# A gated recurrence after linear attention: steps 4 to 7 and the output stage cut in halves of the tokens

## The reference, cut to what matters

```python
# per batch t: x1 = layernorm(x + attention(x)), attention with elu(.)+1 features
def step(c, xt):
    ft = sigmoid(xt @ wf.T + c @ uf.T + bf)
    it = sigmoid(xt @ wi.T + c @ ui.T + bi)
    gt = tanh(xt @ wc.T + c @ uc.T + bc)
    return ft * c + it * gt, None
c_final, _ = lax.scan(step, c0, x1)
h = tanh(einsum('tbi,oi->tbo', x1, wo) + c_final @ uo.T + bo)   # for every tile t
return layernorm(x1 + h)
```

## Time and profile before

| what | value |
|---|---|
| time, median of 3 runs | 106.99 us (106.97 to 107.19) |
| profiled execution, its own time | 107.27 us |
| its span in the trace | 105.2 us |
| PE busy | 92.5 us (88%) |
| DVE busy | 79.5 us (76%) |
| ACT busy | 62.1 us (59%) |
| POOL busy | 40.6 us (39%) |

### The profile page before, as it was taken

How to read it: one execution, slowest core, us unless ns; L and a number is a source line. 1 busy time by engine, 2 the same in 40 slices (tenths; PEclk the granted TensorE clock), 3 DMA queues, 4 the chain that set the end, 5 groups by cost and what they waited for, 6 DMA issues and landing times.

```text
span 105.2 us, 1758 instructions
## 1 busy us (share of the span) xinstructions
PE 92.5 (88%) x570; PEld 78.5 (75%) x570; DVE 79.5 (76%) x225; ACT 62.1 (59%) x115; POOL 40.6 (39%) x59
## 2 busy tenths in 40 slices
PE   6998999889999999999999999999999999991000
PEld 4878779469688968878887888898898899991000
DVE  3325398998999995898689589389592648999950
ACT  1326675349395684676659374374753735799731
POOL 2006277607247149009306604304300002786780
PEclk9999999999999999999999999999999999999855
DMA  1869994000000000000000000000000000034453
GB/s 44 284 250 406 387 386 176 6 0 3 0 0 0 0 0 0 9 0 0 0 0 6 0 0 0 0 0 0 3 0 6 0 0 0 0 142 161 179 211 108
DMA packets 4372, 7.28 MB, mean 69 GB/s; under 512 B 491, under 2 KB 1292, under 8 KB 4364
## 3 DMA queue, kind: packets, MB, share of 16 engines
q1 hardware_dynamic: 3932, 6.85, 17.7%
q10 hardware_dynamic: 432, 0.33, 1.1%
HBM read 5.08 MB, written 2.10 MB: 68 GB/s over the span
## 4 chain that ended last, share of the span: by engine, by line
PE 72%; DVE 18%; POOL 3%; ACT 3%; issue 2%; POOLq 0%; DVEq 0%; ACTq 0%
PE ps_ctx L326 7%; PE ps_k L307 7%; PE ps_ctx L346 6%; PE ps_q L317 5%; DVE stats L663 5%; DVE x L790 4%; PE ps_f L296 4%; PE ps_x L357 3%; POOL rstd L247 2%; DVE x L675 2%; PE ps_f L370 2%; PE ps_f L376 2%; PE ps_c L371 2%; PE ps_c L370 2%; PE ps_c L376 2%; PE ps_i L371 2%
## 5 line engine op out<-in xcount | busy, mean ns | idle before, releaser
L247 POOL TENSOR_TENSOR rstd<-var_eps,minus_half 128x4 f32<-128x4 f32 (+1 forms) x17 | 17.2, 1012 | 22.6 <-DVE var_eps L669 22.3
L276 POOL TENSOR_TENSOR s_lo<-s,s_hi 128x512 fp32r<-128x512 f32 x6 | 7.7, 1291 | 26.7 <-ACT s_hi L591 26.7
L663 DVE BATCH_NORM_STATS2 stats<-x 128x6 f32<-128x256 f32 x32 | 12.3, 425 | 0.3
L675 DVE TENSOR_SCALAR x<-x,stats,rstd 128x128 f32<-128x128 f32 x32 | 11.4, 420 | 0.0
L557 ACT ACTIVATE x<-x,shift,rstd 128x128 f32<-128x128 f32 x21 | 8.9, 480 | 3.6 <-POOL shift L255 3.6
L238 POOL TENSOR_TENSOR k_pair<-k_rows 128x256 f32<-128x256 f32 x8 | 6.3, 785 | 9.9 <-DVE k_rows L697 9.9
L566 ACT ACTIVATE x_hi<-ps_x 128x512 fp32r<-128x512 f32 x8 | 4.8, 597 | 8.6 <-PE ps_x L357 8.6
L326 PEld LDWEIGHTS ps_ctx<-k_rows,x_rows 128*128 128x128 f32 x64 | 8.1, 191 | 2.0 <-issue 1.6
L326 PE MATMUL ps_ctx<-k_rows,x_rows 128*128 128x128 f32 x64 | 8.6, 278 | 0.8 <-DVE x L686 0.5
L307 PE MATMUL ps_k<-wkq,x_cols 128*128 128x128 f32 x64 | 9.3, 293 | 0.0
L537 ACT ACTIVATE k_exp<-ps_k,minus_one 128x512 f32<-128x512 f32 x8 | 5.5, 686 | 6.2 <-PE ps_k L311 6.2
(11 more groups left out here) (161 smaller groups left out, 242.2 us busy)
## 6 DMA issues: line engine op xcount, KB each, us to landing
x_cols<-xt SPq DMA_DIRECT2D x8, 256.0 KB, 7.0
x_rows<-x SPq DMA_DIRECT2D x8, 256.0 KB, 7.2
out<-x SPq DMA_DIRECT2D x7, 256.0 KB, 2.0
wgate<-w_gate SPq DMA_DIRECT2D x1, 384.0 KB, 6.7
out<-x SPq DMA_DIRECT2D x2, 128.0 KB, 1.8
wkq<-w_kq ACTq DMA_DIRECT2D x1, 131.0 KB, 3.4
wvo_in<-w_vo_in ACTq DMA_DIRECT2D x1, 128.0 KB, 3.3
wout<-w_out SPq DMA_DIRECT2D x1, 128.0 KB, 6.9
```

The lines of the kernel that those rows point to most:

```text
L247: nc.gpsimd.tensor_tensor(rstd[:, t, c0:c1], var_eps[:, t, c0:c1], minus_half[:, c0:c1], ALU.pow).then_inc(rstd_ok, 1)
L276: nc.gpsimd.tensor_tensor(s_lo[:, (t - 1) % 2], s[:, (t - 1) % 2].rearrange("p c d -> p (c d)"), s_hi[:, (t - 1) % 2].bitcast(F32), ALU.su ...
L663: st = nc.vector.bn_stats(stats[:, t, c:c + 2].rearrange("p c m -> p (c m)"), tile[:, c:c + 2].rearrange("p c d -> p d c"))
L675: nc.vector.tensor_scalar(x1[:, b, c], x1[:, b, c], mean_of(b, c), rstd[:, b, c:c + 1], ALU.subtract, ALU.mult).then_inc(x1_ok, 1)
```

## The change

Steps 4 to 7 are issued as eight half-steps (256 tokens each); the list `STEPS` gives the order. In it the second half (tokens H to C, with H = C // 2 = 2 chunks) of a step comes later than the first. `step_before(k)` finds the half-step (or whole step) that made the state which step k reads. The output stage's units are now mostly two tiles by half the tokens: four units of the first half, then five of the second half. Units 0 to 3 need only the first half of the last state and are placed among the last half-steps. On every engine the last part of the program is written out. The relevant parts of the diff (definitions that only lose a branch for the removed periods are left out):

```diff
-UNITS = [(t, 0, C) for t in range(T - 1)] + [(T - 1, 0, C // 2), (T - 1, C // 2, C)]
-DVE_NORM = [1, 1, 1, 1, 1, 1, 2, 2, 1]
+STEPS = [(0, 0, C), (1, 0, C), (2, 0, C), (3, 0, C), (4, 0, H), (5, 0, H), (4, H, C), (6, 0, H),
+         (7, 0, H), (5, H, C), (6, H, C), (7, H, C)]
+FULL_PERIODS = 7
+UNITS = [(0, 2, 0), (2, 2, 0), (4, 2, 0), (6, 2, 0), (0, 2, H), (2, 2, H), (4, 2, H), (6, 1, H), (7, 1, H)]
+DVE_NORM = [1, 1, 1, 1, 1, 1, 1, 1, 1]
...
-        x1_hi = sb("x1_hi", [D, 2, N], F32R)
-        x1_lo = sb("x1_lo", [D, 2, N], F32R)
+        x1_hi = sb("x1_hi", [D, T, N], F32R)
+        x1_lo = sb("x1_lo", [D, T, N], F32R)
...
+        unit_bank = [ps_k[:], ps_q[:], ps_ctx[:, 0, :], ps_ctx[:, 1, :], ps_x1[:], ps_k[:], ps_f[:], ps_i[:], ps_c[:]]
...
# SP: one store for a unit
+                sp.dma_start(out[t0:t0 + nt].rearrange("t (p c) d -> p t c d", c=C)[:, :, c0:c0 + H],
+                             part_of(x1, u)).then_inc(stored, 16)
# POOL, behind the seven full periods
+            state_low(4)
+            reciprocal_root(6)
+            reciprocal_root(7)
+            state_low(5)
+            state_low(6)
+            state_low(7)
+            for u in range(len(UNITS)):
+                second_root(u)
                 second_shift(u)
# PE: gate_x_high, gate_x_low and gate_s take ps[:, part], x1_hi[:, t, part], s_hi[:, last, part] of step k
+            gates_x(5)
+            keys_x(7)
+            gate_s(0, 5)
+            key_values(7)
+            gate_s(1, 5)
+            gate_s(2, 5)
+            context(7)
+            gates_x(6)
+            gates_s(6)
+            x1_turned(6)
+            out_x(0)
+            gates_x(7)
+            gates_s(7)
+            x1_turned(7)
             out_x(1)
+            gates_x(8)
+            gates_s(8)
+            gates_x(9)
+            gates_s(9)
+            out_s(0)
+            out_s(1)
+            gates_x(10)
+            out_x(2)
+            gates_s(10)
+            out_s(2)
+            gates_x(11)
+            out_x(3)
+            gates_s(11)
+            out_s(3)
+            for u in range(4, len(UNITS)):
+                out_x(u)
+                out_s(u)
# ACT
+            state_high(4)
+            x1_whole(5)
+            xk_copy(7)
+            gates_tanh(5)
+            gates_tanh(6)
+            x1_high(6)
+            state_high(5)
+            x1_whole(6)
+            gates_tanh(7)
+            state_high(6)
+            x1_high(7)
+            state_high(7)
+            x1_whole(7)
+            gates_tanh(8)
+            gates_tanh(9)
+            out_tanh(0)
+            state_high(9)
+            out_tanh(1)
+            gates_tanh(10)
+            normalise(0)
+            state_high(10)
+            out_tanh(2)
+            normalise(1)
+            gates_tanh(11)
+            out_tanh(3)
+            normalise(2)
+            for u in range(4, len(UNITS)):
+                out_tanh(u)
+                normalise(u - 1)
+            normalise(len(UNITS) - 1)
# DVE
+            def step(k):
+                kept_state(k)
+                new_state(k)
+                next_state(k)
...
+            attention_end(6)
+            key_values(7)
+            normalise(6)
+            kept_state(5)
+            new_state(5)
+            reciprocal_z(7)
+            next_state(5)
+            attention_end(7)
+            step(6)
+            x1_low(6)
+            normalise(7)
+            step(7)
+            x1_low(7)
+            step(8)
+            step(9)
             second_residual(0)
+            second_statistics(0)
+            second_variance(0)
+            state_low(9)
             second_residual(1)
+            second_statistics(1)
+            second_variance(1)
+            step(10)
+            second_normalise(0)
+            state_low(10)
+            second_residual(2)
+            second_statistics(2)
+            second_variance(2)
+            second_normalise(1)
+            step(11)
+            second_residual(3)
+            second_statistics(3)
+            second_variance(3)
+            second_normalise(2)
+            for u in range(4, len(UNITS)):
+                second_residual(u)
                 second_statistics(u)
                 second_variance(u)
+                second_normalise(u - 1)
             second_normalise(len(UNITS) - 1)
```

More of the change, by code:

```diff
@@ L187, in rows_of, with columns, step_before, state @@
             return dram[t].rearrange("(p c) d -> p c d", c=C)
-        def halves(cut):
-            return [slice(0, N // 2), slice(N // 2, N)] if cut else [slice(0, N)]
-        def act_norms(units):
[L195 to L203, removed]
+        def columns(k):
+            _, c0, c1 = STEPS[k]
+            return slice(c0 * D, c1 * D)
+        def step_before(k):
+            t, c0, _ = STEPS[k]
+            return max(j for j in range(k) if STEPS[j][0] == t - 1 and STEPS[j][1] <= c0 < STEPS[j][2])
+        def state(t):
+            return s[:, t % 2].rearrange("p c d -> p (c d)")
+        def blocks(u):
+            t0, nt, c0 = UNITS[u]
+            return [(t, c) for t in range(t0, t0 + nt) for c in (c0, c0 + 1)]
+        def part_of(tile, u, t_first=0):
+            t0, nt, c0 = UNITS[u]
+            return tile[:, t_first + t0:t_first + t0 + nt, c0:c0 + H]
+        def periods():
+            for n in range(FULL_PERIODS):
+                yield n + 1, n, n - 1 if n >= 1 else None, n - 2 if n >= 2 else None
+        def act_norms(units):
+            return sum(len(blocks(u)) - DVE_NORM[u] for u in range(units))
         @block.sync
@@ L272, in _ @@
             for k, a, b, t in periods():
[L273 to L277, removed]
+                if t is not None and t >= 1:
+                    state_low(t - 1)
                 if b is not None:
-                    reciprocal_root(b, b)
-                if k is not None:
-                    key_sums(k)
+                    reciprocal_root(b)
+                key_sums(k)
                 if a == 0:
@@ L394, in gate_s, with gates_x @@
[L394 to L401, removed]
+            def gates_x(k):
+                for g in range(GATES):
+                    gate_x_high(g, k)
+                for g in range(GATES):
+                    gate_x_low(g, k)
+            def gate_s(g, k):
+                ps, _, done = gates[g]
+                u, last, part = GATES + g, (STEPS[k][0] - 1) % 2, columns(k)
+                if k == 1:
+                    pe.wait_ge(split_s_lo, 1)
+                pe.wait_ge(shi_ok[step_before(k)], 1)
+                nc.tensor.matmul(ps[:, part], wgate_hi[:, u], s_hi[:, last, part], start=False, stop=False,
+                                 skip_group_check=True)
+                nc.tensor.matmul(ps[:, part], wgate_lo[:, u], s_hi[:, last, part], start=False, stop=False,
+                                 skip_group_check=True)
+                pe.wait_ge(slo_ok[step_before(k)], 1)
+                nc.tensor.matmul(ps[:, part], wgate_hi[:, u], s_lo[:, last, part], start=False, stop=True,
+                                 skip_group_check=True).then_inc(done, 1)
@@ L412, in out_x @@
                     pe.wait_ge(y_ok, T)
+                if u == 3:
                     pe.wait_ge(y_small_ok, T)
[L414 to L424, removed]
@@ L469, in _ @@
                     continue
[L471 to L481, removed]
+                keys(k)
+                if a == 1:
+                    keys_x(a)
+                if a in (2, 3):
+                    x1_turned(a - 2)
+                queries(k)
                 if t == 0:
@@ L494, in _ @@
                 if t is not None:
[L495 to L500, removed]
+                    gates_x(t)
+                    keys_x(a)
                     gate_s(0, t)
-                if a is not None:
-                    key_values(a)
+                key_values(a)
                 if a == 1:
@@ L699, in key_max, with kept_state @@
                                                ALU.max).then_inc(k_ok, 1)
-            def kept_state(t):
-                dve.wait_ge(f_ok, t + 1)
+            def kept_state(k):
+                t, part = STEPS[k][0], columns(k)
+                dve.wait_ge(f_ok, k + 1)
                 if t == 0:
@@ L776, in _ @@
-                    if a is not None:
-                        reciprocal_z(a)
-                    dve.wait_ge(keep_ok, t + 1)
-                    for h, part in enumerate(parts):
-                        dve.wait_ge(new_ok, t + 1 + h)
-                        nc.vector.scalar_tensor_tensor(s[:, t % 2].rearrange("p c d -> p (c d)")[:, part], keep[:, part], 0.5,
-                                                       new[:, part], ALU.mult, ALU.add).then_inc(s_ok, 1)
-                if b is not None and b >= 1:
-                    x1_low(b)
```

314 lines of the change are left out of this document (164 added, 150 removed).

## The result

The changed kernel takes 109.09 us (median of 4 runs, 108.58 to 109.61), the kernel before 106.98 in the same runs: 2.05% slower, 95% interval 1.3% to 2.8%. In a later group of runs the ratio is 1.026 (1.022 to 1.030). The forecast was 109.2. None of the four runs lies near their median: two took 108.6 and two 109.6. The profiled span grew from 105.2 to 107.8 us.

What follows compares the result with a forecast made beforehand. PE bounds the kernel to about 84.6 us, then DVE and ACT. Late DVE in front and a slower output stage end the span at 107.45, 2.25 longer: 106.99 + 2.25 = 109.2 us, range 108.2 to 110.2 (chance 0.66).

Steps and rivals of the forecast that it cites:

- Prices: Costs taken per half-width instruction: gate matmul 0.125 us, half `new`, `keep` or `s` 0.42, POOL's half `s_lo` 0.75.
- rival 3: Gates on PE: a 256-wide matmul costs nearer 0.20 us; time 110.6 at 0.16, up to 114 at 0.20; chance 0.12.
- Front: Stretch up to the end of half-step 9: DVE becomes late, PE idles 0.94 and 0.92 us.
- checkpoint B: PE ends half-step 9, forecast at 79.6 us, or 77.3 with PE never waiting.
- Rival 2: Front: DVE is not late, PE's waits vanish, everything behind moves by 2.3 us; time 106.9; chance 0.12.
- Middle: Units 0 to 2 between the half-steps: DVE is the slow one, PE is not the limit.
- Checkpoint C: Last state, forecast at 90.68 us against 84.59 before.
- Tail: Units 3 to 8: 2.46 us per unit against 1.66 before; span ends at 107.45, 2.25 longer.
- ring: Output units 3 to 8: variance, root, shift, normalisation, tanh, residual, statistics take 4.93 us for two units, 2.46 for one.
- Rival 1: Output units after the last state: pace stays 1.66 us per unit, time 105.6, faster by 1.3%; chance 0.10.

Runs made afterwards that it cites:

- hi6_early: `tail2` with ACT making s_hi of half-step 6 ahead of the three tanh of half-step 7; 106.16 us, ratio 0.9968 to the kernel before.
- front2: `tail2` with out_x(0) before gates_x(5), and x1_turned(6), x1_high(6), x1_low(6) moved ahead of half-step 6; 106.00 us, ratio 0.9951 to the kernel before.
- best2: `front2` with units 7 and 8 normalised on DVE, x1_turned(7) ahead of out_x(1), s_lo of half-steps 6 and 7 on DVE; 105.07 us, ratio 0.9885.
- late_units: `tail2` with units 0 to 3 no longer among the last half-steps, all nine units following half-step 11; 109.86 us, ratio 1.0327 to the kernel before.
- tail2: Changed kernel with ACT's tail ordered tanh(u), normalise(u - 2) instead of normalise(u - 1); 106.78 us, ratio 0.9997 to the kernel before.
- before_ahead2: Kernel before with ACT's normalisation two tiles behind the tanh instead of three (ACT_AHEAD = 2); 110.91 us, ratio 1.043.

## Why the prediction was right, point by point

**Prices.** The 256-wide matmul at 0.125 was measured at 0.12; rival 3 is out. Half `new` and `s` at 0.42 held everywhere but beside POOL's `s_lo`. POOL's half `s_lo`, taken at 0.75 from `k_pair`, takes 0.72 to 0.74 in the changed kernel.

**Front.** `gates_x(5)` was forecast at 61.43 and starts at 61.55; the low matmuls of half-step 7 at 71.69, measured 71.55 (PE lost 0.6 us there and not 0.92); checkpoint B at 79.6, measured 79.93. The 0.3 there have a cause that the prediction did not have: `s` of half-step 7 at 0.77 instead of 0.42, which pushed `x1_low(7)` and half-step 8. I had called the overlap on POOL free ("no price, but no cover either") and looked only at when results are ready, not at whether POOL and DVE can work beside one another. `hi6_early` shows that cause: with the overlap gone B comes 0.33 us sooner.

**How much the front costs.** Rival 2 said that without the waits everything behind moves by 2.3 us. Closing the two larger ones won 0.69 (`front2`), and `best2` another 0.39, a part of which is the collision with `s_lo`. In `best2` B comes 17.37 us behind `x1_low(5)` and in the changed kernel 18.49, so 1.12 of the 2.3 are shown. The waits do go through to the end, though each repair moved some of it elsewhere. The small waits that make up the rest of the 2.3 were not tried.

**Middle.** Checkpoint C was forecast as a state ready at 90.68; it is ready at 90.56 + 0.42 = 90.98, late by the 0.3 of B. `late_units` shows the trade in it: units 0 to 2 delay the recurrence by 2.0 us.

**Tail.** The ring was forecast at 4.93 us for two units, measured 5.03, since POOL's root takes 1.11 here where it took 1.01. The 0.10 comes from the new order on DVE, which puts `normalise` directly behind the variance, so that POOL's root starts 0.24 us before it ends. In `late_units` the root takes 1.01 us in unit 0, where no `normalise` stands there, and 1.10 or 1.11 in units 1 to 6, where one does. In the kernel before, where a residual or statistics stood there, the root took 1.01 in every unit of four chunks. Last variance 103.23 forecast, 103.62 measured; last normalisation 104.75 and 105.13; end 107.45 and 107.8. `tail2` and `before_ahead2` show the mechanism from both sides, with 2.6 us for the order in the changed kernel. Rival 1, that the old pace of 1.66 stays, is out; even with the ring open the pace is 2.0.

**The size.** The span ended 0.35 us later than forecast, the sum of the two terms above, the 0.3 of the collision and the 0.1 of the ring, with smaller ones of both signs. That the median of the four runs came within 0.1 us of the 109.2 is in part luck: it lies between two clusters 1 us apart, and the later group gave 2.6% where 2.1% was forecast.

**So where did the gain go?** Doing four units early is worth 3.3 us (`late_units` against `tail2`), and the kernel before has the same time as `tail2`. So without these units the cut recurrence is behind the old kernel by that amount. The traces show on which side of the last state. Counted from `x1_low(4)` (54.51 before, 53.92 in `late_units`), up to which both programs are the same, the last state is ready after 30.1 us before and after 34.4 in `late_units`; the output stage behind it takes 20.6 and 19.6. The loss therefore lies wholly in the recurrence, not in the shorter instructions and undivided chains of the output stage. Among its parts are the waits in front and the collision, of which 1.1 us are shown at B; the rest was not split. The ring then took 2.6 us more and made it a loss.

## What to carry to other kernels

When a loop over engines is reordered, work out for each in-order queue the ring of latencies (here variance, root, shift, normalisation, tanh, residual) and divide it by the number of units that the order lets be under way; if that is above the busiest engine's time per unit, the order is the bound. How far one engine normalises behind its tanh is such a number: one place fewer cost 2.6 us here, and 4.3% in the old kernel, with no instruction added. The half-width cut was cheap on PE here and dear in the waits that had been covered by fillers (`out_x(0)` before half-step 5), so a filler that is moved away needs another one in its place.

## What was not expected of the hardware

DVE and POOL get in each other's way in SBUF, but not with every pair of instructions. A DVE instruction with two operands in SBUF (`new`, `s`; 0.42 us alone) took 0.77 us and 0.97 us when it was issued while POOL's `s_lo` ran, and `s` took 0.42 again when POOL's work was moved to another time. The Trainium skill (SBUF — State Buffer, section on the two separate sides) says that VectorE with two SBUF inputs and a GpSimd operation that reads SBUF exclude one another for a whole instruction. For `s_lo` the trace agrees: both long instructions ended 0.28 us behind the end of POOL's (71.11 against 70.83, 75.17 against 74.89), wherever in it they had been issued. For POOL's root, which reads SBUF too, it does not. In the kernel after `new` and `s` run beside it and keep their length:

```profile
69.73 1.11 POOL L268 TENSOR_TENSOR rstd<-var_eps,minus_half 128x4 f32<-128x4 f32 x1 [4.47 <-DVE var_eps L757]
...
69.94 0.42 DVE L803 SCALAR_TENSOR_TENSOR new<-th_i,th_c 128x256 f32<-128x256 f32 x1
...
70.47 0.43 DVE L810 SCALAR_TENSOR_TENSOR s<-keep,new 128x256 f32<-128x256 f32 x1
```

It is the root that gets longer, by what DVE had begun before it: 1.01 us beside a residual, 1.11 when it starts 0.24 us before the end of `normalise`, 1.19 when it starts 0.32 us before the end of `s_lo` or `keep` on DVE (83.41 and 85.42 in the kernel after). DVE's `x1_low`, which has one of its two inputs in PSUM, kept its 0.68 us beside POOL's `s_lo` (both started at 70.81 in the kernel after).

The other surprise is the spread: two executions of one program differ by up to 1.4 us. In the two profiles compared above (0.4 us apart) the whole difference is there after the first 8 us; what makes it was not looked into.
